# The fading factor of a graph attention layer's kept sums moves from SBUF to PSUM

## The reference, cut to what matters

```python
ft = (feat @ W).reshape(n, H, D)
a1 = jnp.einsum('nhd,hd->nh', ft, attn_l)
a2 = jnp.einsum('nhd,hd->nh', ft, attn_r)
e = jax.nn.leaky_relu(a1[src] + a2[dst], negative_slope=ALPHA)
m = jax.ops.segment_max(e, dst, num_segments=n)
ex = jnp.exp(e - m[dst])
s = jax.ops.segment_sum(ex, dst, num_segments=n)
alpha = ex / s[dst]
msg = ft[src] * alpha[:, :, None]
out = jax.ops.segment_sum(msg, dst, num_segments=n)
```

## Time and profile before

| what | us |
|---|---|
| median of 3 runs | 2373.21 (2373.05 to 2374.68) |
| the profiled execution: its own time | 2375.66 |
| the profiled execution: span of the trace | 2373.9 |
| in it, before the edge pass (to the first gather) | 74.4 |
| in it, first gather to end of the last one | 74.4 to 1108.8 |
| in it, after the edge pass (next stage from about 1150) | 1224 |
| busy in the span: PE, DVE, POOL, ACT | 1749, 1396, 1059, 477 |

### The profile page before, as it was taken

One profiled execution on the slowest core, in us unless ns is written; L12 is line 12 of the kernel. 1 busy time (PEld: TensorE's weight loads), 2 busy tenths in 40 slices (PEclk: granted clock), 3 DMA queues, 4 the chain that ended last, 5 costly groups with the idle time before them and its releaser, 6 DMA issues. The chain is left out here.

```text
span 2373.9 us, 34262 instructions
## 1 busy us (share of the span) xinstructions
PE 1749.4 (74%) x8967; PEld 1193.3 (50%) x8967; DVE 1396.0 (59%) x4277; ACT 477.0 (20%) x1077; POOL 1058.5 (45%) x1088
## 2 busy tenths in 40 slices
PE   4477777777777777777344994799999976599970
PEld 3223333333233333333234883499999965488860
DVE  6466666666666666666555214698888845211118
ACT  2100000000000000000231342533333312122212
POOL 1577777777777777775072333000000006222221
PEclk9678888888888888888666996899999986799985
DMA  7455555555555555554324774299400012566744
GB/s 205 106 139 140 140 135 141 140 142 142 142 141 142 140 139 137 139 140 111 93 82 131 240 239 154 49 224 218 99 0 0 0 41 83 160 213 213 213 142 159
DMA packets 255968, 321.43 MB, mean 135 GB/s; under 512 B 64440, under 2 KB 207522, under 8 KB 255767
## 3 DMA queue, kind: packets, MB, share of 16 engines
q1 hardware_dynamic: 198464, 174.84, 27.6%
q0 software_dynamic: 50208, 138.59, 21.8%
q10 hardware_dynamic: 7238, 7.39, 1.1%
HBM read 217.43 MB, written 103.68 MB: 135 GB/s over the span
## 5 line engine op out<-in xcount | busy, mean ns | idle before, releaser
L519 POOL DMA_INDIRECT f_buf<-ftab,scol x806 | 789.1, 979 | 288.5 <-issue 245.3
L602 PE MATMUL ps<-ident,f_left 128*128 128x512 f32 x204 | 181.8, 1046 | 170.2 <-ACT f_left L664 170.2
L919 PE MATMUL ps<-nb_parts,g_counts 128*120 128x256 bf16 x2550 | 305.9, 273 | 0.0
L919 PEld LDWEIGHTS ps<-nb_parts,g_counts 128*120 128x120 bf16 x2550 | 282.9, 133 | 1.9
L611 PE MATMUL ps<-f_diag,f_ones 128*128 128x512 f32 x204 | 186.0, 1067 | 100.6 <-DVE f_diag L753 100.6
L634 PE MATMUL ps<-f_buf,f_hot_e 128*32 128x265 f32 x1632 | 245.7, 393 | 3.1 <-DVE f_buf L789 3.1
L789 DVE TENSOR_TENSOR f_buf<-f_buf,ps 128x1024 f32<-128x1024 f32 x204 | 235.4, 1217 | 17.7 <-ACT ps L673 17.7
L1014 DVE TENSOR_SCALAR g_cell_hot<-nb_table,g_now 128x250 bf16<-128x250 int16 x816 | 230.1, 282 | 0.0
L750 DVE TENSOR_REDUCE ps<-ps 128x8 f32<-128x1024 f32 x51 | 62.9, 1233 | 275.9 <-PE ps L605 275.9
L1013 DVE TENSOR_SCALAR g_src_hot<-nb_table,g_now 128x128 bf16<-128x128 int16 x816 | 202.0, 248 | 27.9 <-PE ps L910 27.6
L1193 POOL MEMSET y_r_half<- 128x25 f32 x1 | 0.1, 121 | 419.0 <-POOLq L873 419.0
(11 more groups left out here) (466 smaller groups left out, 2490.7 us busy)
## 6 DMA issues: line engine op xcount, KB each, us to landing
y_wts<-in_L_ffn_w_dram SPq DMA_DIRECT2D x68, 512.0 KB, 4.0
xs<-zero_rows SPq DMA_DIRECT2D x33, 1032.0 KB, 16.4
x_wts<-in_L_ffn_expert_w_dram SPq DMA_DIRECT2D x84, 256.0 KB, 3.3
xs<-zero_rows SPq DMA_DIRECT2D x51, 403.1 KB, 5.2
f_buf<-ftab,scol POOLq DMA_INDIRECT x806, 2.9
y_xr<-xs SPq DMA_DIRECT2D x34, 258.0 KB, 3.7
x_xr<-xs SPq DMA_DIRECT2D x28, 258.0 KB, 3.2
f_st<-state SPq DMA_DIRECT2D x51, 132.5 KB, 2.4
```

The costliest lines, as they stand in the source:

```text
L519: nc.gpsimd.indirect_dma_start(out=buf[u][:, j, :], out_offset=None, in_=s.ftab, in_offset=bass.IndirectOffsetOnAxis(ap=s.scol[:, b * CB + ...
L602: nc.tensor.matmul(wide[:, w:w + 4, :], left[b.side][:].rearrange("p j h -> p (j h)"), bc(s.ident[:], 1, 4), start=True, stop=False)
L919: last = nc.tensor.matmul(acc[b.side], counts[b.side][:, t, :], s.parts[:, t, n, :], start=t == 0 and n == 0, stop=t == NT - 1 and n == PA ...
```

## The change

The tile `fo` leaves SBUF and becomes two pieces of 8 numbers in PSUM bank 7, behind `mx`. ACT's L669 writes there, and DVE's fading L795 reads one operand from SBUF (`st`) and one from PSUM (`fo`). As bank 7 is in use by DVE, three things go with it: `mask_chunks` (which reads `numbers` from the bank) waits until the fading factor of the batch before its own is written; `merge` waits for that of the next batch instead of its own; and ahead of the loop the second batch's masks are made after the first batch's `batch_tops` instead of before its `chunk_tops`.

```diff
-        bm, zz, gap, fo = two("bm", [W128, HEADS]), two("zz", [W128, 2, HEADS]), two("gap", [W128, HEADS]), two("fo", [W128, HEADS])
+        bm, zz, gap = two("bm", [W128, HEADS]), two("zz", [W128, 2, HEADS]), two("gap", [W128, HEADS])
...
         ex = ps[:, 7, W128:W128 + CB * HEADS].rearrange("p (j h) -> p j h", h=HEADS)
+        fo = [ps[0:W128, 7, 256 + W8 + p * HEADS:256 + W8 + (p + 1) * HEADS] for p in range(2)]
...
             def fade(b):
                 act.wait_ge(look_ready, b.count())
                 act.wait_ge(merged, b.count(2))
-                nc.scalar.activation(fo[b.side][:], gap[b.side][:], ACT.Exp).then_inc(fo_ready, 1)
+                nc.scalar.activation(fo[b.side], gap[b.side][:], ACT.Exp).then_inc(fo_ready, 1)
...
             def mask_chunks(b):
                 dve.wait_ge(crow_in[b.side], b.by_side())
+                dve.wait_ge(fo_ready, b.count(1))
...
-            def merge(b):
+            def merge(b, nxt):
                 dve.wait_ge(st_in, b.count() * 16 - 16 * OPEN)
-                dve.wait_ge(fo_ready, b.count())
+                dve.wait_ge(fo_ready, (nxt or b).count())
                 by_head = st[b.side][:, 0:RW - 1].rearrange("p (h e) -> p h e", e=HW)
-                nc.vector.tensor_tensor(by_head, by_head, bc(fo[b.side][:], 2, HW), ALU.mult)
+                nc.vector.tensor_tensor(by_head, by_head, bc(fo[b.side], 2, HW), ALU.mult)
...
                 mask_chunks(b0)
                 mask_batch(b0)
-                mask_chunks(b1)
                 chunk_tops(b0)
                 batch_tops(b0)
+                mask_chunks(b1)
...
-                    merge(b)
+                    merge(b, nxt)
```

## The result

The changed kernel takes **2352.33 us** (median of 5 runs, 2349.03 to 2359.26) against 2373.21 us before (5 runs, 2371.06 to 2376.35): a ratio of 0.9913, 95% interval 0.9895 to 0.9932, or 21 us less. The forecast was 2349, with 2344 to 2360 as its range.

A forecast was written before the change was run, and what follows sets the result against it. The prediction took POOL's queue of 16 gathers a batch as the bound. Freeing 49 lengthened gathers gave 24.8 us, all other parts nothing: 2373.2 - 24.8 = 2348.4, called 2349 us, range 2344 to 2360.

The forecast's parts named there:

- What bounds: Edge pass: POOL's queue of 16 gathers a batch sets the pace; POOL waits for nobody, other engines have slack.
- The gathers' lengthening: Edge pass: 49 gathers beside the fading are lengthened, and the change removes all of it, 24.8 us.
- the first three fadings: Start of the edge pass: their gathers were said to be lengthened by 1.0 to 1.25 us, the other 46 by some 0.46.
- Who holds the gather: Fading behind the chunk masks: its two SBUF operands stall the gather, queueing time included; forecast's chance 0.82.
- The rival that L737 holds the port: Chunk masks hold the port too, so only 9.3 us are gained: 2364 us; chance 0.08.
- the rival that the PSUM operand frees nothing: Fading still claims the port with one SBUF operand: 8.3 us slower, 2381.5 us; chance 0.06.
- The fading's own time: Fading on DVE, one operand now from PSUM: +0.02 us on 0.41 us.
- The wait in bank 7: Chunk masks wait for the next batch's factor: 0.15 us later per batch, hidden in DVE's idle time.
- ACT's slack: ACT's wait for gathers at L664, 3.96 us a batch, shrinks by no more than 0.15 us, so POOL stays the bound.
- The tail: From the last gather to the next stage: nothing changes; ACT takes the gather up 2.0 us after its end.
- The moved masks of the second batch: Ahead of the loop, from 88.41 to near 100.4 us: delay of some 0.6 us falls into DVE's idle time, costing nothing.
- the last two merges: Last two batches: the fading waits some 0.35 us more, hidden as L798 waits for PE anyway; costs nothing.

The follow-up runs named there:

- e2: Kernel before with one VectorE drain between chunk masks and fading, both fading operands still in SBUF: 2568.3 us against 2568.2 on chip 8 (0.9995).
- e7: The kernel of e2 run again on chip 8: 2577.0 us against 2576.0 for the kernel before (0.9999).
- p3: The kernel of e2 plus seven drained POOL clears per batch: 2717.1 us, 1.0550 of the kernel before without them.
- e4: Kernel before with the fading's product made twice, first into a spare tile: 2569.1 us against 2568.2 on chip 8 (0.9995).
- e5: Changed kernel plus one product per batch behind the masks, both operands in SBUF: 2575.6 us, 1.0002 of the kernel before on chip 8.
- e6: Changed kernel plus the added product of e5 with its second operand in PSUM: 2577.5 us, 1.0006 of the kernel before on chip 8.
- e1: Kernel before with only the change's order and waits, factor left in SBUF: 2570.1 us against 2568.2 on chip 8 (1.0005).
- p5: The kernel of e1 plus seven drained POOL clears per batch, on chip 0: 2775.8 us against 2376.5 for the kernel before (1.1688).
- p2: Changed kernel plus seven drained POOL clears per batch: 2717.3 us, 1.0555 of the kernel before without them.
- p4: Kernel before with the fading moved between L783 and the messages, plus seven drained POOL clears per batch: 2721.3 us, 1.0559 of the kernel before.

## Why the prediction was right

- **What bounds:** right for the chip on which before and after were measured: POOL waited for nobody in either. It is not so on every chip, which the profile of before could not show.
- **The gathers' lengthening, 24.8 us in the forecast:** 23.8 us by busy time from 100 to 1110 us, 23.9 by the pass's length. Of the missing 1.0 us, 0.3 is four gathers beside L781 and L785 (the forecast had allowed for the first of these). Most of the rest is that free gathers take 0.947 us on average in both kernels, where the forecast took their median, 0.946, 787 times. Its words that the first three fadings cost 1.0 to 1.25 us misread the rows: of the first four batches the second costs 0.41 us and the other three that much (gathers of 2.04, 1.36, 2.20 and 1.95 us). The sum doesn't use it.
- **Who holds the gather:** the charge to the instruction with two SBUF operands, queueing included, was an inference from three odd gathers and a clean one. It is now shown three ways: e2, e7 and p3 (144 gathers under the masks, none lengthened once the fading can't be queued), e4 (more of it, more lengthening), e5 against e6 (operand's place alone). The rival that L737 holds the port is out; the rival that the PSUM operand frees nothing fell with the first profile after.
- **The Trainium skill:** its sentence that a VectorE instruction with two SBUF inputs contends with a GpSimd one that reads SBUF holds here. Its note beside it, that a tensor_tensor was not seen to stall DMAs with GpSimd's descriptors, does not (e5 against e6: 33.8 us over 806 gathers). The same section (SBUF — State Buffer, Who interferes with whom) says that issue order decides who blocks; the trace agrees and adds where the order begins, in the queue.
- **The fading's own time:** forecast 0.43 us, measured 0.41.
- **The wait in bank 7:** mis-sized. Forecast 0.15 us later per batch, from a gap of 0.04 us between an ACT end and a DVE start; the gap here is 0.15 us (601.46 to 601.61), so L739 starts 0.53 us after the factor's argument instead of some 0.3. It cost nothing, since DVE's 5 us of waiting for PE lie behind it: that part held.
- **ACT's slack:** from 3.96 us to 3.70 (184.9 / 50). Forecast at most 0.15 less; it is 0.26 less, still far from binding.
- **The tail:** forecast unchanged, measured 1.5 us longer, at a lower granted clock. With the early start that makes 22.9 against 24.8 for the execution; the medians' 20.9 lies below both, and the interval of the ratio (16 to 25 us) holds them all.
- **The moved masks of the second batch and the last two merges:** nothing, as forecast; the last-but-one fading is followed by a 1.2 us wait for PE in both kernels (L800 at 1104.95).

Still open: what holds back the sums on chip 8. ACT's and POOL's waits there end 0.68 us apart, from something the profile can't name. ACT's copy of the sums starts 4.1 to 5.3 us after PE's last recorded matmul (medians of e1 to e7), and 0.11 us after it in the kernel before and in p5.

## What to carry to other kernels

When a queue of indirect DMAs on POOL sets the pace, list the durations of its instructions: here the outlier once per period came from a VectorE instruction with two SBUF operands, and its end told which. Three things took it away, wholly or nearly: one operand in PSUM, another place in the program, or a drain that keeps that instruction from standing queued behind a long one. The drain is one line and gave the same time here (p3 against p2); the PSUM operand is the one that doesn't depend on phase, since with the other two a gather that starts while the instruction itself runs is still held (16 in p3, 23 in p4). And ask first whether POOL waits: where it does, none of this shows in the time.

## What was not expected of the hardware

- A VectorE instruction with two SBUF operands keeps a gather waiting before it starts: up to 1.03 us ahead of its own start in e1, and never when a drain stands between it and the instruction ahead. In the kernels with such an instruction behind the masks, gathers that started up to 0.21 us after the masks' start could still get by, and from 0.17 us on they could be held.
- The gather needs 0.82 to 0.84 us from the end of what holds it to its own end, in all 396 lengthened gathers of the fourteen profiles, whatever it had waited.
- Two SBUF operands are not the only form that holds a gather. L783 (under its number in each kernel) is a tensor_scalar of 128 x 128 numbers with a single SBUF operand and a constant, and 29 of the 396 end 0.82 us behind it, 14 of them in p5, where it is L788:

```profile
692.10 0.23 DVE L788 TENSOR_SCALAR f_arg<-f_z 128x128 f32<-128x128 f32 x1
692.15 1.00 POOL L520 DMA_INDIRECT f_buf<-ftab,scol  x1 [0.30 <-issue]
```

  It runs for 0.23 us and costs a gather 0.05 us at most. Neither the prediction nor any experiment looks into it: what was tested is products and the fading.
- The same kernel took 2373 and 2377 us in two series of runs (the second on chip 0) and 2568 to 2576 in three on chip 8, with the difference in the edge pass (20.5 against 23.7 us a batch).
